# Third cross attention: the rows' bias from the query projection, one step for both query factors, and the last keys' values on two row sets

## What is computed

```python
def _L2_xattn_ref(x, tab_x, tab_g, tab_b, vid_g, vid_b, Wq, Wk, Wv, q_g, q_b, k_g, k_b, Wo, bo):
    ...
    HEADS = 12
    DHEAD = 64
    INNER = HEADS * DHEAD
    ...
    kv_in = layernorm(tab_x, tab_g, tab_b)
    q = layernorm(layernorm(x, vid_g, vid_b) @ Wq, q_g, q_b)
    k = layernorm(kv_in @ Wk, k_g, k_b)
    v = kv_in @ Wv
    q, k, v = (split(q) * scale, split(k), split(v))
    sim = jnp.einsum('bhid,bhjd->bhij', q, k)
    attn = jax.nn.softmax(sim, axis=-1)
    out = jnp.einsum('bhij,bhjd->bhid', attn, v)
    ...
    return out @ Wo + bo
x = x + _L2_xattn_ref(_layernorm(x, axis=-1), ctx_1024, ...)
```

## Time and profile before

| | us |
|---|---|
| median of 3 runs | 3643.74 |
| lowest and highest run | 3635.27, 3648.31 |
| span of the profiled execution | 3638.3 |
| PE busy in it | 3295.5 |
| DVE, ACT, POOL busy in it | 2210.1, 1355.6, 1140.8 |

### The profile page before, as it was taken

How to read it: one execution, slowest core, us unless ns; L and a number is a source line. 1 busy time by engine, 2 the same in 40 slices (tenths; PEclk the granted TensorE clock), 3 DMA queues, 4 the chain that set the end, 5 groups by cost and what they waited for, 6 DMA issues and landing times.

```text
span 3638.3 us, 94656 instructions
## 1 busy us (share of the span) xinstructions
PE 3295.5 (91%) x39948; PEld 2769.7 (76%) x39948; DVE 2210.1 (61%) x5328; ACT 1355.6 (37%) x3333; POOL 1140.8 (31%) x1717
## 2 busy tenths in 40 slices
PE   7988739997998979999999879989999999998996
PEld 6876638546986758888888757877888878887895
DVE  5766552356676147666666567745444448888557
ACT  5863101233221214444444533313223236665211
POOL 6667215122003434333333242300000025554102
PEclk9989859999997989999999989979999999999997
DMA  5620139461003321111111100003112111112000
GB/s 162 183 82 3 62 140 280 139 216 48 3 3 123 92 73 53 48 48 50 51 48 42 56 1 3 3 15 113 63 64 93 64 40 49 51 49 66 3 3 27
DMA packets 211286, 246.62 MB, mean 68 GB/s; under 512 B 19412, under 2 KB 191184, under 8 KB 207920
## 3 DMA queue, kind: packets, MB, share of 16 engines
q1 hardware_dynamic: 203376, 230.34, 20.0%
q0 software_dynamic: 7488, 10.23, 1.5%
HBM read 221.46 MB, written 18.61 MB: 66 GB/s over the span
## 4 chain that ended last, share of the span: by engine, by line
PE 76%; DVE 12%; issue 4%; ACT 3%; POOL 3%; DMA 1%; SPq 0%; ACTq 0%; POOLq 0%; DVEq 0%
PE psum L189 46%; PE psum L3656 11%; PE psum L991 2%; PE psum L3906 2%; PE psum L963 2%; PE psum L3115 1%; PE psum L3216 1%; PE psum L3184 1%; PE psum L3896 1%; PE psum L976 1%; DVE g_xn L258 1%; DVE l2a_ss L1659 1%; POOL l0a_ms L1191 1%; PE psum L3125 1%; PE psum L3116 1%
## 5 line engine op out<-in xcount | busy, mean ns | idle before, releaser
L245 POOL TENSOR_SCALAR g_rs<-g_mv 128x4 f32<-128x4 f32 x24 | 5.0, 207 | 777.1 <-DVE g_mv L378 776.6
L3656 PE MATMUL psum<-l2f_hhi,l2f_whi 128*128 128x512 f32 x512 | 199.3, 389 | 0.0
L3656 PE MATMUL psum<-l2f_hlo,l2f_whi 128*128 128x512 f32 x512 | 199.2, 389 | 0.0
L3656 PE MATMUL psum<-l2f_hhi,l2f_wlo 128*128 128x512 f32 x512 | 199.2, 389 | 0.0
L189 PE MATMUL psum<-l2x_kT,l2x_Qp 128*128 128x257 f32 x768 | 179.3, 383 | 2.7 <-ACT g_xn L3539 2.6
L3710 DVE CAST l2f_hhi<-l2f_tmp 128x512 fp32r<-128x512 f32 x96 | 41.0, 427 | 201.7 <-ACT l2f_tmp L3773 200.6
L189 PEld LDWEIGHTS psum<-l2x_kT,l2x_Qp 128*128 128x128 f32 x768 | 142.0, 191 | 22.0 <-issue 3.2
L3773 ACT ACTIVATE l2f_tmp<-psum,g_cols 128x512 f32<-128x512 f32 x64 | 44.2, 690 | 240.1 <-PE psum L3656 240.1
L389 DVE TENSOR_TENSOR g_x<-g_x,psum 128x256 f32<-128x256 f32 x128 | 53.0, 414 | 127.8 <-PE psum L189 124.6
L3539 ACT ACTIVATE g_xn<-psum,l2x_sm 128x257 f32<-128x257 f32 x192 | 89.0, 473 | 90.6 <-DVE l2x_sm L3445 90.6
L4103 ACT ACTIVATE l3x_P<-psum,l3x_sm 128x257 f32<-128x257 f32 x256 | 117.9, 480 | 2.8 <-DVE l3x_sm L4025 2.6
(11 more groups left out here) (877 smaller groups left out, 10882.6 us busy)
## 6 DMA issues: line engine op xcount, KB each, us to landing
l2f_raw<-L2f_h SPq DMA_DIRECT2D x64, 512.0 KB, 3.2
l0f_w<-L0f_w SPq DMA_DIRECT2D x23, 1024.0 KB, 7.7
l0x_ctxT<-ctxT SPq DMA_DIRECT2D x64, 257.0 KB, 2.8
l1x_ctxT<-ctxT SPq DMA_DIRECT2D x64, 257.0 KB, 6.1
l0x_ctok<-ctx SPq DMA_DIRECT2D x64, 256.0 KB, 3.0
l1x_ctok<-ctx SPq DMA_DIRECT2D x64, 256.0 KB
l2x_cT<-ctxT SPq DMA_DIRECT2D x64, 256.0 KB, 2.7
l2x_tok<-ctx SPq DMA_DIRECT2D x128, 128.0 KB, 2.9
```

The source lines that it names most:

```text
L3656: t = e.matmul(z, a, b, start=c == 0 and u == 0, stop=c == 7 and u == 2)
```

## The change

- **Rows' bias.** The six matmuls with `kb` for each group go. Instead the preparation makes 12 more columns of the query projection: `gb` = `kb` times the query gain (and times the query offset) on POOL, their column sums by six PE matmuls (`gs`, behind router round 13), a centred copy on POOL, twelve PE matmuls with the turned query weights `wqT` (three more DMAs, 768 KB) in `pe_end`, and an ACT copy into `wq[:, :, 768:780]`. The second half of the query projection has 396 columns instead of 384. DVE makes the bias `rq` from these columns with one scalar_tensor_tensor of 12 columns before it writes `qn`. `rbt` is no longer a take of a PSUM bank.
- **Both factors in one step.** `gain` and `shift` (128 x 6) are products made once on POOL. DVE's six pieces now write `qk` directly from PSUM; `qT` and POOL's product L3304 go. DVE waits for the previous group's spread to have been read by PE (for the first group, for the turning L3137 that reads the same buffer).
- **Last keys' values on two row sets.** `VT` is 40 x 384 instead of 12 x 768: heads 0 to 5 on partitions 0 to 7, heads 6 to 11 on partitions 32 to 39 (8 rows each, filled by four DMAs instead of three). The 12 matmuls now have 8 rows and alternate between the row sets and column halves. `Rt` is written by two DVE instructions of 8 x 512, and the turning of `ptl` becomes two plain matmuls with 8 columns of weights each, into partitions 0 to 7 and 32 to 39.

```diff
@@ ClipWeights.pool
+        w.wait_ge(self.small_all)
+        for u, name in enumerate(("L2_xattn_q_g", "L2_xattn_q_b")):
+            o, n = CAT[name]
+            e.tensor_tensor(self.gb[:, :, 12 * u:12 * u + 12], self.kb[:], K.cols[:, o:o + n].unsqueeze(2).to_broadcast([128, 6, 12]),
+                            ALU.mult).then_inc(*self.gb_ok.up())
+        w.wait_ge(self.gs_ok.at(2))
+        w.wait_ge(self.gb_ok.now())
+        e.tensor_tensor(self.gb[:, :, 0:12], self.gb[:, :, 0:12], self.gs[:].unsqueeze(1).to_broadcast([128, 6, 12]),
+                        ALU.subtract).then_inc(*self.gm_ok.up())
@@ ClipWeights.pe
+        if n == 13:
+            w.wait_ge(self.gb_ok.at(2))
+            matmuls(e, take("gs", 0)[:, 0:24], [(K.ones[:], self.gb[:, ch, :]) for ch in range(6)]).then_inc(*self.gs_ps.up())
@@ ClipWeights.pe_end
+        w.wait_ge(self.gm_ok.at(1))
+        z, prev = self.banks.take(("wqk", 0))
+        self.freed(w, prev)
+        for c in range(2):
+            t = matmuls(e, z[:, 12 * c:12 * c + 12], [(self.wqT[:, ch, c * 128:(c + 1) * 128], self.gb[:, ch, 0:12]) for ch in range(6)])
+        t.then_inc(*self.wqk_ps.up())
@@ l2_xattn, sp: rows
-                for n in range(3):
-                    load(e, r_in[i % 2], VT[i % 2][4 * n:4 * n + 4, 256 * n:256 * n + 256], vts[4 * i:4 * i + 4, 256 * n:256 * n + 256])
+                for r, a, m, n in ((0, 0, 0, 256), (4, 256, 256, 128), (32, 0, 384, 128), (36, 128, 512, 256)):
+                    load(e, r_in[i % 2], VT[i % 2][r:r + 4, a:a + n], vts[4 * i:4 * i + 4, m:m + n])
@@ pe: queries, spread0, turn_p, heads
-                    t = matmuls(e, zz[n][:, 0:384], [(xT[:, c, i * 128:(i + 1) * 128], wq[:, c, n * 384:(n + 1) * 384])
-                                                     for c in range(2)])
+                    m = slice(n * 384, (n + 1) * 384 + 12 * n)
+                    t = matmuls(e, zz[n][:, 0:384 + 12 * n], [(xT[:, c, i * 128:(i + 1) * 128], wq[:, c, m]) for c in range(2)])
...
-                z = take("rbt", i)
-                w.wait_ge(qT_ok.at(2 * i + 2))
-                matmuls(e, z[:, 0:12], [(qT[:, ch, :], kb[:, ch, :]) for ch in range(6)]).then_inc(*rbt_ps.up())
-                w.wait_ge(qk_ok.at(i + 1))
+                w.wait_ge(qk_ok.at(2 * i + 2))
                 spread(i, 0)
...
-                    e.transpose(take("pl", i)[0:12, 0:128], ptl[i % 2][:].rearrange("p n j -> p (n j)"), ident[:]).then_inc(*pl_ps.up())
+                    z, tails = take("pl", i), ptl[i % 2][:].rearrange("p n j -> p (n j)")
+                    for g in range(2):
+                        t = e.matmul(z[half[g], 0:128], tails[:, 4 * g:4 * g + 8], ident[:], start=True, stop=True)
+                    t.then_inc(*pl_ps.up())
...
-                for ch in range(6):
-                    for par in range(2):
-                        o, h, d = head(ch, par)
-                        t = e.matmul(o, VT[i % 2][:, d], Rt[:, h % 4], start=False, stop=True, skip_group_check=True)
-                    if ch % 3 == 2:
-                        t.then_inc(*o_ps.up())
+                for v in range(3):
+                    for g in range(2):
+                        for par in range(2):
+                            o, h, d = head(3 * g + v, par)
+                            t = e.matmul(o, VT[i % 2][half[g], 128 * v + 64 * par:128 * v + 64 * par + 64], Rt[half[g], h % 4],
+                                         start=False, stop=True, skip_group_check=True)
+                        if v == 2:
+                            t.then_inc(*o_ps.up())
@@ pool: scaled
-                if b % 4 == 0:
...
-                    e.tensor_tensor(qk[:], qT[:], K.cols[:, o:o + n].unsqueeze(2).to_broadcast([128, 6, 128]),
-                                    ALU.mult).then_inc(*qk_ok.up())
@@ dve: apply_q, variances, turn_p
+                    e.scalar_tensor_tensor(out=rq[:], in0=banks.of(("q", i, 1))[:, 384:396], scalar=mq[:, 2:3], in1=cb[:], op0=ALU.mult,
+                                           op1=ALU.add).then_inc(*rq_ok.up())
...
-                            t = e.tensor_scalar(qT[:, ch, :], banks.of(("qt", i, n))[:, v * 128:(v + 1) * 128],
-                                                K.col("L2_xattn_q_g", ch), K.col("L2_xattn_q_b", ch), ALU.mult, ALU.add)
-                        t.then_inc(*qT_ok.up())
+                            t = e.tensor_scalar(qk[:, ch, :], banks.of(("qt", i, n))[:, v * 128:(v + 1) * 128],
+                                                gain[:, ch:ch + 1], shift[:, ch:ch + 1], ALU.mult, ALU.add)
+                        t.then_inc(*qk_ok.up())
...
-                    e.tensor_tensor(Rt, z.unsqueeze(2).to_broadcast([12, 4, 4, 32]),
-                                    rmod[:].unsqueeze(1).unsqueeze(3).to_broadcast([12, 4, 4, 32]), ALU.mult).then_inc(*Rt_ok.up())
+                    for r in half:
+                        z = banks.of(("pl", i))[r, 0:128].rearrange("p (h q) -> p h q", h=4)
+                        e.tensor_tensor(Rt[r], z.unsqueeze(2).to_broadcast([8, 4, 4, 32]),
+                                        rmod[r].unsqueeze(1).unsqueeze(3).to_broadcast([8, 4, 4, 32]), ALU.mult).then_inc(*Rt_ok.up())
```

More of the change, by code:

```diff
@@ L2829, in __init__ @@
         self.wgT = T("wgT", [128, 6, 257], self.early)
+        self.wqT, self.kb, self.gb = T("wqT", [128, 6, 256], self.early), T("kb", [128, 6, 12], self.early), T("gb", [128, 6, 24], self.early)
+        self.gs = T("gs", [128, 12], self.early)
+        self.gb_ok, self.gs_ps, self.gs_ok, self.gm_ok, self.wqk_ps, self.wqk_ok = (S("gain_bias"), S("gain_sum_ps"), S("gain_sum"),
+            S("gain_centred"), S("wqk_ps"), S("wqk"))
         self.banks = Banks(K.bank[3:8])
@@ L2840, in ready @@
     def ready(self, w):
-        for v in (self.wv_ok, self.wkT_ok, self.G_ok, self.bb_ok):
+        for v in (self.wv_ok, self.wkT_ok, self.G_ok, self.bb_ok, self.wqk_ok):
             w.wait_ge(v.at(0))
@@ L2850, in sp @@
         load(e, self.small, self.bo[:], A["L2_xattn_bo"].rearrange("(a n) -> a n", a=1))
-        load_rows(e, self.small, self.wq, A["L2x_q"])
+        load_rows(e, self.small, self.wq[:, :, 0:768], A["L2x_q"])
         load_rows(e, self.small, self.kb, A["L2x_kb"], split=6)
+        load_rows(e, self.small, self.wqT, A["L2x_qT"])
         load(e, self.small, self.rmod[:], A["rowmod"])
@@ L2934, in freed @@
             w.wait_ge({"wv": lambda: self.wv_ok.at(n + 1), "bvm": lambda: self.bvm_ok.at(1), "G": lambda: self.G_ok.at(n + 1),
-                       "c0": lambda: self.c0_ok.at(1), "bo": lambda: self.brow_ok.at(1), "bias": lambda: self.bb_ok.at(1)}[what]())
+                       "gs": lambda: self.gs_ok.at(2), "wqk": lambda: self.wqk_ok.at(1), "c0": lambda: self.c0_ok.at(1), "bo": lambda: self.brow_ok.at(1), "bias": lambda: self.bb_ok.at(1)}[what]())
     def act(self, e):
@@ L2968, in act @@
             e.activation(GG[:, c, 128:129], z[:, 256:257], ACT.Copy, scale=2 / 768).then_inc(*self.G_ok.up())
+        w.wait_ge(self.gs_ps.at(1))
+        e.activation(self.gs[:], prep.of(("gs", 0))[:, 0:12], ACT.Copy, scale=1 / 768).then_inc(*self.gs_ok.up())
+        copy_act(e, self.cb[:], prep.of(("gs", 0))[:, 12:24]).then_inc(*self.gs_ok.up())
         w.wait_ge(self.c0_ps.at(1))
@@ L2972, in act @@
         copy_act(e, self.brow[:], prep.of(("bo", 0))[0:1, 0:256]).then_inc(*self.brow_ok.up())
+        w.wait_ge(self.wqk_ps.at(1))
+        copy_act(e, self.wq[:, :, 768:780], prep.of(("wqk", 0))[:, 0:24].rearrange("p (c n) -> p c n", c=2)).then_inc(*self.wqk_ok.up())
         w.wait_ge(self.bb_ps.at(1))
@@ L2995, in l2_xattn @@
         Pc, oT = [T(f"Pc{k}", [128, 2, 12, 128]) for k in range(2)], T("oT", [128, 6, 128])
-        vts, VT, ptl, fold = T("vts", [64, 768]), [T(f"VT{k}", [12, 768]) for k in range(2)], [T(f"ptl{k}", [128, 3, 4]) for k in range(2)], T("fold", [128, 32])
+        vts, VT, ptl, fold = T("vts", [64, 768]), [T(f"VT{k}", [40, 384]) for k in range(2)], [T(f"ptl{k}", [128, 3, 4]) for k in range(2)], T("fold", [128, 32])
         flat, wf = K.xn[:].rearrange("p i d -> p (i d)"), wk[:].rearrange("p c m -> p (c m)")
@@ L3002, in l2_xattn @@
         kk = [wf[:, 512 * k:512 * (k + 1)].rearrange("p (t s) -> p t s", t=2) for k in range(2)]
-        Rt = wf[0:12, 1024:1536].rearrange("p (h j q) -> p h j q", h=4, j=4)
+        Rt = wf[0:40, 1024:1536].rearrange("p (h j q) -> p h j q", h=4, j=4)
+        half = [slice(0, 8), slice(32, 40)]
         kkt = qk[0:64, 0:2, :]
@@ L3246, in pool @@
                 e.memset(VT[c][:], 0.0).then_inc(*zero.up())
+            columns = lambda name: K.cols[:, CAT[name][0]:CAT[name][0] + 6]
+            e.tensor_tensor(gain[:], columns("L2_xattn_q_g"), columns("L2_xattn_k_g"), ALU.mult).then_inc(*gain_ok.up())
+            e.tensor_tensor(shift[:], columns("L2_xattn_q_b"), columns("L2_xattn_k_g"), ALU.mult).then_inc(*gain_ok.up())
             w.wait_ge(ahead.c0_ok.at(0))
@@ L3390, in variances @@
                     i = b // 4
```

(6 more changed lines are left out.)

39 lines of the change are left out of this document (16 added, 23 removed).

## The result

The changed kernel took 3624.57 us by its median (3616.26 to 3635.42, six runs), the kernel before 3644.63 us beside it: ratio 0.995, with a 95% interval from 0.9934 to 0.9966. By the ratio it is some 18 us faster (12 to 24 by the interval); the two medians differ by 20.1 us. A second comparison on another occasion (the last set of experiments) gave 0.9958, 0.9942 to 0.9975. The forecast was 3628 us.

A forecast was written before the change was run, and what follows sets the result against it. PE was taken to bound the block (busy 554.68 of 560 us). The terms, 12.5 + 9.9 - 5.6 - 0.6 - 0.75 = 15.5 us, taken from the median 3643.74 gave 3628 us, range 3616 to 3640.

The forecast's parts named there:

- Rows' bias: Removing the six `kb` matmuls (1.33 us) gains 0.82 us per steady group, 12.5 us together; `heads` then waits for ACT's copy.
- Last keys: Twelve last-key matmuls per group on two row sets: 0.84 us instead of 1.46, gain 0.62 us, 9.9 us over 16 groups.
- Last probabilities: Turning of `ptl` as two narrow matmuls between full-size ones: loss of 0.35 us per group, 5.6 us over 16 groups.
- Query projection: Twelve more columns in two matmuls: loss of 0.04 us per group, 0.6 us in all.
- Preparation: Feed-forward block: `gs` matmuls behind a router round lose 0.75 us once; twelve `wqk` matmuls, 2.8 us, hidden before the token lists.
- The three more transfers: SP's extra 768 KB in the preparation, ahead of other transfers: put at 0, with a bound of 2 us lost.
- First group: DVE's six pieces wait for the turning: 0.6 us lost, `rq` adds 0.2, against 1.5 us of `kb`: gain 0.7 us.
- B: Rival, chance 0.20: exponentials and copies move up with PE, no new wait in `heads`; 1.33 us per steady group, 3621 us.
- C: Rival, chance 0.20: row sets don't overlap at this size; last keys still cost 1.46 us, 3638 us, no measurable change.
- D: Rival, chance 0.04: DVE late in the softmax, its divisions stretched by POOL's `toklo`; PE waits 1.86 us per group, 3658 us.
- my sign that DVE's division would no longer be stretched: In the profile after, DVE's division L3454 would no longer be stretched once in a group; stretched more under D.
- E: Rival, chance 0.04 beyond the forecast's range: preparation not hidden, up to 6 us, 3634 us; a later router or lists, 3640 or above.

The follow-up runs named there:

- the last set of experiments: Changed kernel plus 40-column single turning, query banks freed by halves and ACT's first copy before the exponentials: 3609.56 us, beside the unaltered changed kernel at 3623.64 us.
- the kernel with two steps: Changed kernel with DVE writing the turned queries with their own gain and offset and POOL multiplying by the key gain again: 3649.5 us, timed once.

## Why the prediction was right

*Rows' bias.* The step was that PE would meet ACT's first copy in `heads`, and that the gain would be 0.70 us plus what the copy gained by DVE's three-column step no longer running beside POOL. Both halves are shown: the wait is there, the step fell from 0.58 to 0.16 us, and giving POOL its product back, alone, made the wait 0.44 us. I took 0.82 us; at this place it is 1.07 (1.34 less 0.10 and 0.17). The wait came out at 0.11 us of idle time, below the 0.2 to 0.6 that I had named as the sign. The first copy takes 0.50 us and not half of 0.88, while the 0.1 us from ACT to PE held. The assumed 0.42 us arrived whole, and the delay I had allowed against it (a second `Rt`, `rq`, POOL beside the division) cost nothing there. Missing from the sum was the 0.15 us at the probabilities' turning: `rq` holds the query banks longer, and I had looked only for DVE's lateness in the softmax, not for who takes those banks next. With it the term is 0.92.

*Last keys.* Forecast 0.84 us for the twelve, measured 0.81. The price from steps in pairs, taken from a row of another block, held.

*Last probabilities.* Forecast a loss of 0.35 us, measured 0.41: 0.21 at the turning and 0.20 at its two neighbours, and these 0.20 stay under the 0.28 us that the fold of `rbt` set as the bound. The sign (0.45 us from the turning to the scores) read 0.32, since half of the loss lies beside it.

*Query projection.* 0.04 us, as measured (2.58 to 2.62).

*Preparation.* Forecast 0.75 us at the `gs` matmuls. The distance between the two router sums around them:

```profile
1167.98 0.46 PE L1765 MATMUL psum<-l1f_cnt,g_ones 128*128 128x24 f32 x2
...
1170.03 1.41 PE L189 MATMUL psum<-l1f_next_gb,g_ones 128*128 128x24 f32 x12
1171.28 0.38 PE L1765 MATMUL psum<-l1f_cnt,g_ones 128*128 128x24 f32 x2
```

3.30 us, and 2.55 before: 0.75. That the figure came out so exactly is luck: `gs` took 1.25 us and not 1.4, and the `wgT` matmuls ahead of it ran at a granted clock of 0.79. In the second profile of the changed kernel the distance is 3.15 us, a loss of 0.60. It is not a fixed price. In the kernel with two steps the same distance is 4.34 us, because the `wgT` matmuls ahead of `gs` took 2.92 us there instead of 1.92 (1.60 before). The stretches over these matmuls, in the kernel before and in the one with two steps, show a granted clock of 0.97 and of 0.51, the higher and the lower level (2.4 and 1.2 GHz):

```profile
1159.50:1161.50 2.00, 1.60 (x7) 1.09 (x7) 1.61 (x6) 0.34 (x2) 0.00 (x0) 0.97 0.00 0
```

```profile
1169.60:1172.60 3.00, 3.00 (x11) 2.44 (x10) 1.91 (x7) 0.00 (x0) 0.00 (x0) 0.51 0.00 0
```

At the lower level the round was full before `gs` came. The token lists stayed where they were: 5.66 us from the ranks to the lists, 5.57 before. PE's idle time ahead of them shrank from 4.24 to 0.78 us, so 3.5 us of the cover are used, where the forecast had 2.8 for the twelve matmuls (they took 3.1). The three more transfers, which I had put at nothing with a bound of 2 us, moved nothing that PE waits for: from the token lists to the block's first query projection it is 149.75 us, and 149.72 before.

*First group.* DVE's six pieces start at 1346.51, 0.43 us behind the start of L3167 at 1346.08, as forecast; from the first query projection to the first spread it is 13.16 us and was 13.91, a gain of 0.75 against the 0.7 in the sum; both at a granted clock of 1.00.

*The rivals.* B (no new wait in `heads`) fell by the wait itself, though it came nearer than I thought: of its 1.33 us, 1.07 arrived, and 0.17 of what is missing is the wait. C (row sets don't overlap) fell by 0.81 us and by the count of records in flight. D (DVE late in the softmax) fell, since no wait of PE names it. But my sign that DVE's division would no longer be stretched did not come either: three of them took 1.93 us in the tick ahead, now beside POOL's `toklo`, where they took 2.11 beside the product. E was right in that the cover was nearly used up, and stayed inside its bounds.

For a steady group the forecast's terms make 0.82 + 0.62 - 0.35 - 0.04 = 1.05 us, and they measured 0.92 + 0.65 - 0.41 - 0.04 = 1.12. So the sum of 15.5 us against some 18 measured is mostly the term of the rows' bias, too small by 0.1 us for each group, and not a wrong mechanism. The timed runs alone, with 12 to 24 us, could not have told 15.5 from 18; the distances in the traces do.

## What to carry to other kernels

When PE is nearly full, price a removal by the distance between starts, then look for the wait behind it: who has to read the bank that PE now wants earlier, and what stands ahead of that reader on its own engine. When an instruction is put on a reader of a PSUM bank, look up who takes that bank next, however far away; moving the instruction within the reader changes nothing, releasing the bank in parts does. Where a trace repeats a pattern many times, compare the period and not the span: here it resolved 0.02 us for each group, while the same code ahead of the change took 1124 us in one execution and 1132 in another.
